# The four sums of weight quadrants of the gate and up products, moved from VectorE to GpSimd from the fourth stage on

## The reference

```python
def attention(x, ctx):                    # x layer-normalised
    Q = x @ Wq.T + bq;  K = ctx @ Wk.T + bk
    return softmax(Q @ K.T / sqrt(1024)) @ ctx

def feed_forward(x):                      # x layer-normalised
    Wg = NF4_CODE[gate_q] * scale         # 16 fixed values, one scale per block of 64
    Wu = NF4_CODE[up_q] * scale
    Wd = NF4_CODE[down_q] * scale
    return (silu(x @ Wg.T) * (x @ Wu.T)) @ Wd.T

x = x + attention(layernorm(x), ctx)
x = x + feed_forward(layernorm(x))
```

## Time and profile before

| | |
|---|---|
| median of 3 runs | 1913.26 us (1912.08 to 1914.53) |
| time of the profiled execution | 1912.7 us |
| its span | 1910.9 us |
| TensorE busy | 1896.5 us of the span (99%) |
| VectorE busy | 1630.9 us (85%) |
| ScalarE busy | 1440.5 us (75%; it has nothing to do after about 1670 us) |
| GpSimd busy | 423.4 us (22%) |
| granted TensorE clock | full, in all slices but the last |
| attention part | up to about 363 us |
| gate and up part | about 363 to 1397 us (its first slots lie between matmuls of the attention part) |
| down part | 1397 us to the end |

### The profile page before, as it was taken

One profiled execution on the slowest core, in us unless ns is written; L12 is line 12 of the kernel. 1 busy time (PEld: TensorE's weight loads), 2 busy tenths in 40 slices (PEclk: granted clock), 3 DMA queues, 4 the chain that ended last, 5 costly groups with the idle time before them and its releaser, 6 DMA issues.

```text
span 1910.9 us, 29498 instructions
## 1 busy us (share of the span) xinstructions
PE 1896.5 (99%) x9758; PEld 963.4 (50%) x9758; DVE 1630.9 (85%) x2652; ACT 1440.5 (75%) x2678; POOL 423.4 (22%) x629
## 2 busy tenths in 40 slices
PE   9999999999999999999999999999999999999999
PEld 4487888644444444444444444444444444444444
DVE  7978999869889899899898898898799899996963
ACT  3887776588998988988988988988989999900000
POOL 2023353301111121121121121121245343311110
PEclk9999999999999999999999999999999999999999
DMA  9348999955554565454464455465568998974462
GB/s 357 71 87 192 260 258 286 301 157 129 118 146 127 115 153 129 117 156 123 114 157 120 112 158 128 111 152 141 148 174 233 240 228 221 257 246 139 148 237 83
DMA packets 437641, 326.15 MB, mean 171 GB/s; under 512 B 371680, under 2 KB 371952, under 8 KB 435568
## 3 DMA queue, kind: packets, MB, share of 16 engines
q1 hardware_dynamic: 393280, 170.55, 39.6%
q0 software_dynamic: 44032, 153.65, 24.7%
q10 hardware_dynamic: 176, 0.07, 0.0%
HBM read 154.31 MB, written 82.31 MB: 124 GB/s over the span
## 4 chain that ended last, share of the span: by engine, by line
PE 77%; ACT 9%; DVE 6%; issue 3%; SPq 0%; DMA 0%; DVEq 0%; POOL 0%; ACTq 0%
PE ps L2329 40%; PE ps L2372 26%; PE ps L1695 7%; ACT sq L362 3%; ACT sq L358 2%; PE ps L1663 2%; PE ps L1730 2%; DVE w L378 1%; ACT tail L2403 1%; DVE tail L2479 1%; ACT halves L430 1%; PE ps L1634 0%; DVE halves L446 0%; ACT tail L2414 0%; DVE T L1139 0%
## 5 line engine op out<-in xcount | busy, mean ns | idle before, releaser
L2329 PE MATMUL ps<-T,wS 128*128 128x512 f16 x4704 | 1017.7, 379 | 5.0 <-DVE ps L2431 2.5
L2329 PEld LDWEIGHTS ps<-T,wS 128*128 128x128 f16 x4704 | 459.5, 98 | 560.1 <-issue 6.8
L362 ACT ACTIVATE sq<-sq 128x512 f32<-128x512 f32 x898 | 515.9, 626 | 0.0
L378 DVE SCALAR_TENSOR_TENSOR w<-sq,w 128x512 f32<-128x512 f32 x590 | 426.3, 723 | 102.0 <-ACT sq L362 91.9
L358 ACT ACTIVATE sq<-q 128x512 f32<-128x512 int32 x560 | 341.0, 631 | 51.4 <-DVE w L378 50.6
L2372 PE MATMUL ps<-T,tail 128*128 128x512 f16 x1584 | 344.8, 379 | 1.6 <-DVE tail L2445 1.1
L2372 PEld LDWEIGHTS ps<-T,tail 128*128 128x128 f16 x1584 | 154.8, 98 | 189.0 <-DVE tail L2445 1.5
L446 DVE SCALAR_TENSOR_TENSOR halves<-w,halves 128x512 f16<-128x512 f32 x240 | 163.0, 688 | 15.1 <-POOL halves L437 8.0
L2267 POOL DMA_DIRECT2D keep_h<-tail x196 | 106.7, 544 | 283.4 <-DVE tail L2479 283.2
L2372 PE MATMUL ps<-T,wS 128*128 128x512 f16 x768 | 168.4, 379 | 0.0
L430 ACT CAST halves<-w 128x512 f16<-128x512 f32 x200 | 123.8, 620 | 42.4 <-DVE w L378 31.6
(11 more groups left out here) (245 smaller groups left out, 1898.5 us busy)
## 6 DMA issues: line engine op xcount, KB each, us to landing
keep_h<-tail POOLq DMA_DIRECT2D x196, 256.0 KB, 2.5
tail<-keep_h POOLq DMA_DIRECT2D x66, 512.0 KB, 4.5
wS<-keep_h POOLq DMA_DIRECT2D x32, 512.0 KB, 4.4
T<-in_x SPq DMA_DIRECT2D x13, 1024.0 KB, 8.3
q<-in_L_ffn_up_q POOLq DMA_DIRECT2D x52, 256.0 KB, 3.0
q<-in_L_ffn_gate_q POOLq DMA_DIRECT2D x48, 256.0 KB, 3.6
q<-in_L_ffn_down_q POOLq DMA_DIRECT2D x42, 256.0 KB, 4.3
keep_x<-T SPq DMA_DIRECT2D x38, 256.0 KB, 4.4
```

What stands on the lines that cost most here:

```text
L362: nc.scalar.activation(place, place, ACT.Square, bias=b, scale=a).then_inc(un.s_act, 1)
L378: nc.vector.scalar_tensor_tensor(out=out, in0=square_place(un, u, i - 1), scalar=FACTORS[i - 1][1], in1=un.w[:, buf, :], op0=ALU.add, op1= ...
L2329: last = nc.tensor.matmul(ps[:, bank, :], un.wS[:, z % SLOTS, a, kt, :], t.Tp[side][product][:, :, b, kt, :], start=fresh and n == 0, stop ...
```

## The change

- From stage 3 on (POOL_SUMS = 3) the sums are GpSimd instructions: sums_of is called in GpSimd's program, behind loads_due of the phase after the one in which VectorE is to finish the unit (self.sums). In stages 0 to 2 VectorE still makes them.
- SUM_3 is now made first, after the second unit of a stage; SUM_1 and SUM_2 after the third, SUM_4 after the fourth. Each waits for the last factor of its unit, and for the low halves of the pieces that used the buffer before.
- The first step of a unit waits for the sums that read the buffer which it overwrites (sums_read): for units 1 to 3 of a stage, all sums of the stage before; for the first unit, all but SUM_4.
- In the fourth unit of a stage, the casts of SUM_1 and SUM_2 come after ScalarE's steps 6 and 8 (before: 4 and 6), their low halves after VectorE's steps 3 and 4 (before: 2 and 3).
- The planner: the sums are no steps of VectorE from stage 3 on (for stages 0 to 2, SUM_1 with SUM_2 is one), the period of deal has eight VectorE steps fewer, and ScalarE may take two steps more than its share in a phase (before: one). Its fixed quotas and CREDIT, FULL stay.

```diff
+SUM_ORDER = (SUM_3, SUM_1, SUM_2, SUM_4)
+POOL_SUMS = 3
...
     first = PIECES * (u // 4) if u < GATE_UP_UNITS else GATE_UP_PIECES + u - GATE_UP_UNITS
     wait(dve, un.s_wlo, last_piece_in(buf, first) + 1)
-    wait(dve, un.s_add, 4 * min(u // 4, STAGES))
+    sums_read(dve, un, u)
...
-def combine(nc, dve, un, stage, out, left, right, op):
-
-    wait(dve, un.s_wlo, last_piece_in(out, PIECES * stage) + 1)
-    wait(dve, un.s_add, 4 * stage)
-    nc.vector.tensor_tensor(un.w[:, out, :], un.w[:, left, :], un.w[:, right, :], op).then_inc(un.s_add, 1)
+def sums_read(eng, un, u):
+
+    if u < GATE_UP_UNITS:
+        wait(eng, un.s_add, 4 * (u // 4) - (1 if u >= 4 and u % 4 < 3 else 0))
+    else:
+        eng.wait_ge(un.s_add, 4 * STAGES)
+
+
+def sum_done(eng, un, stage, out):
+
+    eng.wait_ge(un.s_add, 4 * stage + SUM_ORDER.index(out) + 1)
+
+
+def combine(add, eng, un, stage, out, left, right, op):
+
+    wait(eng, un.s_wlo, last_piece_in(out, PIECES * stage) + 1)
+    add(un.w[:, out, :], un.w[:, left, :], un.w[:, right, :], op).then_inc(un.s_add, 1)
+
+
+def sums_of(add, eng, un, u):
+
+    stage, i = u // 4, u % 4
+    if i == 1:
+        eng.wait_ge(un.s_fac, STEPS * (u + 1))
+        combine(add, eng, un, stage, SUM_3, A11, A21, ALU.subtract)
+    elif i == 2:
+        eng.wait_ge(un.s_fac, STEPS * (u + 1))
+        combine(add, eng, un, stage, SUM_1, A21, A22, ALU.add)
+        sum_done(eng, un, stage, SUM_1)
+        combine(add, eng, un, stage, SUM_2, SUM_1, A11, ALU.subtract)
+    elif i == 3:
+        eng.wait_ge(un.s_fac, STEPS * (u + 1))
+        sum_done(eng, un, stage, SUM_2)
+        combine(add, eng, un, stage, SUM_4, A12, SUM_2, ALU.subtract)
...
         for i in range(STEPS):
             yield factor(nc, dve, un, t, u + 3, i)
-            if i in (2, 3):
-                yield piece_lo(nc, dve, un, t, z + i - 1)
+            if i in (3, 4):
+                yield piece_lo(nc, dve, un, t, z + i - 2)
...
         for i in range(OPS):
             yield square(nc, act, un, u + 3, i)
-            if i in (4, 6):
-                yield piece_hi(nc, act, un, t, z + i // 2 - 1)
+            if i in (6, 8):
+                yield piece_hi(nc, act, un, t, z + i // 2 - 2)
...
+                    if d in at_end:
+                        self.sums.setdefault(phase + 1, []).append(at_end[d])
...
-        steps = (2 * (4 * STEPS + 4 + PIECES), 2 * (4 * OPS + PIECES))
+        steps = (2 * (4 * STEPS + PIECES), 2 * (4 * OPS + PIECES))
...
-                dealt[first + n] = now[0], now[1] + 1
+                dealt[first + n] = now[0], now[1] + 2
...
             loads_due(HIDDEN_PHASE + k)
+            for u in PLAN.sums.get(HIDDEN_PHASE + k, ()):
+                sums_of(nc.gpsimd.tensor_tensor, pool, un, u)
```

More of the change, by code:

```diff
@@ L424, in piece_hi @@
         else:
-            act.wait_ge(un.s_add, 4 * stage + buf - SUM_1 + 1)
+            sum_done(act, un, stage, buf)
     else:
@@ L555, in __init__ @@
             act_unit(u + 2, {})
-            act_unit(u + 3, {4: (z + 1,), 6: (z + 2,)})
+            act_unit(u + 3, {6: (z + 1,), 8: (z + 2,)})
         for z in range(GATE_UP_PIECES - 4, GATE_UP_PIECES):
@@ L604, in __init__ @@
         self.dealt = self.deal()
-        self.turns, self.loads = {}, {}
+        self.turns, self.loads, self.sums = {}, {}, {}
+        at_end = {fac[u, STEPS - 1]: u for u in range(4 * POOL_SUMS, GATE_UP_UNITS)}
         at_lo, loaded = {n: z for z, n in lo.items()}, Q_RING
```

27 lines of the change are left out of this document (14 added, 13 removed).

## The result

The changed kernel takes 1939.47 us (median of 4, 1937.55 to 1940.17), beside 1913.89 us before: a ratio of 1.0123, 95% interval 1.01 to 1.0147. I had forecast 1916.0. The profiled execution took 1940.17 us with a span of 1938.4 us, 27.5 us more than before. The page's first part, against the earlier trace rows: GpSimd has its 100 instructions more, VectorE 100 fewer, and yet VectorE is busy for 7 us longer.

What follows compares the result with a forecast made beforehand. TensorE, busy 1896.5 of 1910.9 us, bounds the kernel; VectorE and ScalarE only have deadlines. On 1912.7 us, +1.8 +3.1 -1.7 -0.5 = +2.7 gives 1915.4, or 1916.0 us by the median, range 1911 to 1929 us.

Steps and rivals of the forecast that it cites:

- the forecast's own signs of being wrong: Forecast is wrong if odd stages each have a gap over 0.5 us, or if stage 3 has none.
- step 4: ScalarE's copies come later behind extra squares: stage 3 +3.1 us, stage 5 -1.7, stage 7 -0.5, stage 27 nothing.
- step 3: GpSimd's sums hold VectorE instructions with two SBUF operands; 0.2 us in each odd stage 9 to 25, 1.8 us.
- Step 1: 100 sum instructions leave VectorE, 60 us of its queue, worth nothing by itself as VectorE would mostly wait longer.
- Step 2: A GpSimd sum takes 1.26 us alone, 1.72 beside VectorE; 126 to 172 us more, and its queue has room.
- The walk through stage 19: Part of step 3: Z adds at 1091.2 and 1093.3, each 0.5 us ahead of TensorE's slot, so nothing lost.
- the bound of 8: Upper bound of step 3: all three holds at 1.72 us, 0.9 us in each odd stage 9 to 25.
- Step 5: ScalarE's later casts and VectorE's low halves: no wait for SUM_1 and SUM_2, 0.6 us to spare.
- The 1930 us of the holds: Rival: holds on VectorE stop TensorE at odd stages' Z adds, 1.5 us each in ten stages; 1930 us, chance 0.24.
- The late sums: Rival: GpSimd's sums come late for ScalarE's casts, so its copies are late, 1 us a stage; 1923 us, chance 0.12.

Runs made afterwards that it cites:

- y8s: Kernel y8 with GpSimd's sums over one column of 512, plain copies for the transposing DMAs: 1915.5 us, ratio 1.0003.
- e3: Changed kernel with plain copies for the transposing DMAs, its sums made by VectorE at the slots where GpSimd issued them: 1935.7 us.
- e1: Changed kernel with plain copies for the transposing DMAs, GpSimd's sums over one column of 512, same order, waits and plan: 1928.7 us.
- v12: Changed kernel, plain copies for transposes, ScalarE's dealt share due plus nothing in stages 4 and 5, minus one in 26 and 27: 1926.1 us.
- e5: Changed kernel with plain copies for the transposing DMAs, all sums made by VectorE in its own stream and counted there: 1927.3 us.
- b2: Kernel before, plain copies for transposes, with only the first two sums' casts and low halves two steps and one step later: 1928.8 us.
- y8f: Kernel y8 with each GpSimd sum replaced by 32 fills of 16 columns that read nothing, plain copies for transposes: 1918.8 us.
- b1: Kernel before, plain copies for transposes, with only ScalarE's dealt share at due plus two instead of plus one: 1932.0 us.
- y8: Changed kernel, plain copies, old cast and low-half places, share plus one (plus nothing at ends), smaller credit, two more VectorE operations a stage counted: 1930.4 us.
- y7: Kernel y8 with a leaner ScalarE share: minus one in the first period, VectorE's count three operations a stage more, credit as before: 1937.1 us.

## Why the prediction was wrong

The time lies 23.5 us above the forecast, and the forecast's own signs of being wrong came true: the odd stages have gaps over 0.5 us. Steps 4 and 3 failed. In TensorE's timeline step 4 is some 13 us of the miss (stage 27 8.7, stage 5 4.3, slow stretches included) and step 3 some 4; 5.8 us lie outside gate and up and were walked in no step.

**Step 1 (VectorE's freed 60 us is worth nothing)**: right for the order of before. In y8s, which is close to it, VectorE is rid of the 60 us and the time is the same (ratio 1.0003). In the changed order the 60 us are worth 7.0 us (e3 against e1).

**Step 2 (a sum takes 1.26 to 1.72 us)**: about right, 1773 ns on average over the 75 between 700 and 1390 us, just above the upper end.

**Step 3 (holds)**: that sums hold factors is shown by e1 and the fills. The walk through stage 19 failed. It put the first Z add 0.5 us ahead of its slot; measured, TensorE waited 0.62 us. The hold is not why: without it 0.47 us stay (e1), since VectorE's wait for the square takes the hold up. What the walk had wrong are the squares. It let the third factor start between 2.5 and 3.1 us ahead of the slot, counted from the time of before, and took the early end; measured, it starts 2.35 us ahead. And the last factor waits 0.23 us for its own square, a wait that the walk put at nothing. So the gaps are those of a Z add moved behind two factors that wait for ScalarE, with 0.15 us each from the sums. The eight gaps and their matmul ends are some 6 us where I had 1.8, and I had them under holds; that 6 lies within the bound of 8 is luck. What the sums' length and reading do cost in this order, 6.3 us, falls in other places: the gap at stage 2's V add goes from 1.64 to 0.23 us with one column, that in stage 27 from 7.26 to 5.53.

**Step 4 (ScalarE's copies)**: this is the step that failed most. In stage 3 I had 3.8 us of gap at the copies. Measured are 1.5 there and 2.7 in stage 2 at VectorE's adds (2.5 of it at line 2472, the V add, VectorE's add to P7's result), which I hadn't walked; that the sum, 4.2, is near is luck in part. In stage 5 I had the gaps gone but for 0.3; it was 2.75, and 1.9 of slow matmuls. In stage 27 I had nothing with a bound of 2; it was 7.27 and 1.4. I set ScalarE's idle time against the extra squares, 7.7 us ahead of stage 5 and 3.3 us ahead of stage 27, as if ScalarE could use it. It didn't. The same stretches of TensorE's slots in the changed kernel, ScalarE alone, against the earlier trace rows:

```profile
505.20:541.50 36.30, 31.10 (x60) 1.00 0.53 124
541.50:577.80 36.30, 34.92 (x67) 1.00 0.53 138
1353.30:1371.30 18.00, 14.11 (x26) 1.00 0.49 148
```

It is idle for 5.2 and 1.4 us, 6.6 of the 7.7, and for 3.9 us where it was 3.3. Ahead of stage 5 that is waiting for VectorE's factors, which free its buffers (5.1 us), and for a unit to cast (1.3 us). Right behind the last of these stretches it also waited 3.19 us for a sum of GpSimd:

```profile
1374.72 1.14 ACT L461 CAST halves<-w 128x512 f16<-128x512 f32 x2 [3.19 <-POOL w L429]
```

v12 shows the size, 8.9 us for both ends, with 3.8 us of new gaps in the down part. The 35.2 us that ScalarE waits for VectorE's sums at line 2495 are not the reason: e1 has them too, e5 has 0.2 us, and the two take the same time within 1.3 us.

**Step 5 (later casts)**: no wait for GpSimd's sums in stages 9 to 25, as said. What it left out is the low half's place: moved back, it lets one step more stand ahead of the Z add. b2 gives that edit alone 16.4 us, of which 5.4 are gaps at these adds. I had counted what moves to the front of the copies, and not what then stands in front of the Z add on the other engine, though that row stood in my own walk.

**The rivals.** The 1930 us of the holds came nearest and had the right place, the Z adds of the odd stages, for the wrong reason: in this order holds and late sums are 6.3 us together, and only 0.15 us a stage there. The late sums are 3 us where they can be seen alone (y8f). No rival was an order that costs 16 us without GpSimd. What stays open: why b1 and b2, 19.5 and 16.4 us alone, are 14.9 us together with the sums' new order (e5), and why stage 27 waits 5.53 us in e1 and 1.28 and 0.80 in e5 with almost the same squares ahead. I have no count that ranks them.

## What to carry to other kernels

Where two engines feed each other step by step, what decides whether a third engine's deadline is met is which instructions stand ahead of the one that it waits for, and whether one of them waits itself. Moving two casts and two low halves a stage by two places cost 16.4 us here, while taking 60 us of work off VectorE gained nothing. List for each deadline what waits directly ahead of it before and after, on both engines, and don't set idle time of an engine against new work before you know what it idles for. A hold close ahead of a deadline costs (from the held pair's start to stage 19's Z add it is 1.1 us more in y8 than in y8s); ahead of an instruction that waits for something else it may cost nothing, like the pair of 3.10 us in the changed kernel. Split an edit of several parts on the chip, since a part that pays inside the whole (the later casts) can be a loss alone, and the other way round.

## What the runs showed of the hardware

A GpSimd sum with 128x512 float32 operands in SBUF holds VectorE's instruction of two SBUF operands to its end: a pair of factors took 3.10 to 3.17 us in place of 1.42 beside two sums. In stage 19 the pair ended 0.55 us after the sums. Fills of the same tile, 32 in a row for 1.54 us, held nothing: the factors took 689 ns on average and 694 at most. Sums over one column, which read too, held nothing that can be seen either (688 ns, at most 694). First steps (line 393) are held too when they fall beside a sum, 802 ns on average in the changed kernel, 683 in e1.

TensorE's granted clock fell after its longer gaps. Windows of the changed kernel, TensorE alone (length, busy (matmuls), clock, DMA share, GB/s), around the gaps of 2.75 and 7.27 us:

```profile
570.00:600.00 30.00, 27.25 (x119) 0.94 0.49 105
1380.00:1400.00 20.00, 12.42 (x51) 0.83 0.49 117
```

With the two levels of 1.2 and 2.4 GHz, means of 0.94 and 0.83 are 3.6 and 6.8 us at the lower one. They cost 1.9 and 1.4 us; a part of the 6.8 us lies in the gap itself, where nothing is to be lost. The rows behind the gaps of 0.62 us show no such excess (72.68 us for 336 matmuls), and neither does this one of y7, behind 2.86 us:

```profile
883.98 72.68 PE L2366 MATMUL ps<-T,wS 128*128 128x512 f16 x336 [2.86 <-DVE ps L2468]
```

So a gap of some microseconds can have a second price behind it, which my bounds in step 4 didn't hold, and doesn't always have it.
